# Half of the first feed-forward chunk placed inside the last attention step, with key-tile sums on GpSimd in every step

## The reference

```python
qkv = einsum('bsd,ed->bse', x, w_qkv) + b_qkv
scores = einsum('bhqd,bhkd->bhqk', q, k) / sqrt(32) + causal
out = softmax(scores) @ v                       # heads joined, 512 wide
x = layernorm(x + out @ w_out.T + b_out)
hidden = relu((x @ sign(up_weight).T) * up_scale)           # 2048 wide
x = layernorm(x + (hidden @ sign(down_weight).T) * down_scale * output_scale)
```

## Time and profile before

| | us |
|---|---|
| three runs | 776.65, 772.4, 778.32 |
| median | 776.65 |
| the profiled execution, device time | 774.34 |
| its span | 772.6 |

### The profile page before, as it was taken

How to read it: one execution, slowest core, us unless ns; L and a number is a source line. 1 busy time by engine, 2 the same in 40 slices (tenths; PEclk the granted TensorE clock), 3 DMA queues, 4 the chain that set the end, 5 groups by cost and what they waited for, 6 DMA issues and landing times.

```text
span 772.6 us, 11683 instructions
## 1 busy us (share of the span) xinstructions
PE 722.7 (94%) x4032; PEld 505.2 (65%) x4032; DVE 450.5 (58%) x1086; ACT 317.2 (41%) x631; POOL 354.4 (46%) x487
## 2 busy tenths in 40 slices
PE   6899999999999999999979889999999999999993
PEld 4788665655656556565544544788778787878882
DVE  4176495785967859678567751633294339334515
ACT  5211365654655546555546565432232222122210
POOL 4461467394673946739423502632353235223333
PEclk9999999999999999999999999999999999999998
DMA  6976464435544355452677331313012001000101
GB/s 231 296 208 177 110 174 124 136 105 163 150 132 132 108 157 148 115 133 88 174 206 261 109 123 58 120 32 119 14 41 95 28 1 41 15 1 12 44 1 54
DMA packets 44619, 85.71 MB, mean 111 GB/s; under 512 B 4880, under 2 KB 13584, under 8 KB 44432
## 3 DMA queue, kind: packets, MB, share of 16 engines
q1 hardware_dynamic: 35536, 79.72, 34.2%
q10 hardware_dynamic: 9024, 5.24, 2.4%
HBM read 55.33 MB, written 29.36 MB: 110 GB/s over the span
## 4 chain that ended last, share of the span: by engine, by line
PE 71%; DVE 19%; issue 3%; DMA 3%; POOL 2%; ACT 2%; SPq 0%; ACTq 0%; POOLq 0%
PE ps_heads L1045 9%; PE ps_proj L1087 7%; DVE heads_sb L835 7%; PE ps_proj L947 7%; PE ps_score L1104 6%; PE ps_unit L1063 6%; PE ps_unit L1087 5%; PE ps_sum L1039 5%; DVE maxes L813 5%; PE ps_unit L983 4%; PE ps_heads L1104 3%; PE ps_unit L1015 3%; PE ps_sum L1104 3%; PE ps_score L1015 2%; PE ps_score L983 2%
## 5 line engine op out<-in xcount | busy, mean ns | idle before, releaser
L655 POOL TENSOR_TENSOR hid_low<-hid_raw,hid_high 128x512 fp32r<-128x512 f32 x64 | 85.1, 1330 | 175.0 <-DVE hid_high L886 171.9
L711 ACT ACTIVATE probs<-ps_unit 128x512 f32<-128x512 f32 (+3 forms) x216 | 101.9, 490 | 88.4 <-PE ps_unit L1015 85.0
L619 POOL TENSOR_SCALAR_AFFINE_SELECT probs<-probs 128x128 f32<-128x128 f32 x256 | 73.1, 298 | 113.0 <-ACT probs L711 108.9
L711 ACT ACTIVATE probs<-ps_score 128x512 f32<-128x512 f32 (+3 forms) x155 | 75.2, 498 | 77.0 <-PE ps_score L1015 75.6
L886 DVE CAST hid_high<-hid_raw 128x512 fp32r<-128x512 f32 x64 | 27.1, 424 | 125.4 <-ACT hid_raw L766 125.2
L809 DVE CUSTOM_DVE_ANT_0 ps_unit<-ps_unit,causal 128x512 f32<-128x512 f32 (+3 forms) x162 | 80.1, 511 | 32.5 <-PE ps_unit L983 31.5
L1045 PE MATMUL ps_heads<-probs,v_rows 128*32 128x512 f32 (+3 forms) x768 | 80.3, 502 | 11.8 <-DVE heads_sb L837 11.8
L983 PE MATMUL ps_unit<-stack 96*128 96x512 f32 (+3 forms) x246 | 83.8, 354 | 5.7 <-DVE maxes L809 2.5
L1015 PE MATMUL ps_unit<-stack 98*128 98x512 f32 (+2 forms) x216 | 78.4, 366 | 4.1 <-DVE maxes L809 4.0
L613 POOL TENSOR_TENSOR parts<-qk_full,parts 128x512 fp32r<-128x512 f32 x32 | 41.3, 1289 | 64.7 <-ACT parts L690 64.4
L835 DVE RECIPROCAL heads_sb<-ps_sum 128x128 f32<-128x128 f32 x64 | 60.8, 950 | 9.2 <-PE ps_sum L1039 9.2
(11 more groups left out here) (195 smaller groups left out, 1478.0 us busy)
## 6 DMA issues: line engine op xcount, KB each, us to landing
stack<-qk_parts SPq DMA_DIRECT2D x96, 256.0 KB, 4.6
qk_parts<-parts SPq DMA_DIRECT2D x32, 512.0 KB, 2.9
v_all<-h_even ACTq DMA_DIRECT2D x16, 256.0 KB, 3.8
v_rows<-v_all SPq DMA_DIRECT2D x8, 512.0 KB, 4.3
heads_t<-heads_sb SPq DMA_DIRECT2D x16, 256.0 KB, 3.4
raw<-up_w SPq DMA_DIRECT2D x8, 512.0 KB, 3.9
x_tile<-x_rows SPq DMA_DIRECT2D x16, 256.0 KB, 5.5
raw<-down_w SPq DMA_DIRECT2D x8, 512.0 KB, 3.4
```

Source lines behind the costliest of these rows:

```text
L655: nc.gpsimd.tensor_tensor(hid[1][:, (HM * s + n) % 3, :], hid_raw[:, n % 2, :], hid[0][:, (HM * s + n) % 3, :].bitcast(FP32), ALU.subtract ...
L711: nc.scalar.activation(probs[:, (NP * s + n) % RING, 0:width], bank(what, s, n)[:, off:off + width], ACT.Exp, scale=SCALE).then_inc(s_exp, 1)
```

## The change

Chunk 0 is worked in two rounds of two token tiles (256 tokens) each. Round 0 has its 16 up and 16 down tiles inside step 7, from slot 16 to 49.3, with its own small buffers for the hidden tiles (`hid0`); round 1 starts at the old place. To make room, the first two tiles' output projection moves into the end of step 6, the layer norm of chunk 0 to the front of step 7, the weights' loads are ordered up and down in turns, and step 7's scores have three PSUM banks up to piece 16 and two after it (four before). GpSimd adds the four full key tiles in steps 6 and 7 too. In step 6 the fetch of the heads, w_out and x stand ahead of the projection block (1, 3), whose twelve matmuls go from slots 11.9 to 17.1 to slots 19.4 to 26.2, with its store at 29.4 and its return at 31.9 (before: 19.9 and 22.2). The down weights are written into `down_sb` from above, as before, but their last two loads wait for the added tiles only.

```diff
@@ -36,10 +36,10 @@
 PAIRED = [13, 13, 19.6, 19.6, 28, 28, 36, 36, 44, 44, 52, 52]
 PAIRED_NORM = [19.7, 19.71, 19.72, 19.73, 52.05, 52.06, 52.07, 52.08]
-ALONE = [[11.2, 13.5, 15.7, 18.3, 24, 28, 31.5, 36, 39.5, 43, 46.5, 50.3],
+ALONE = [[11.2, 13.5, 15.7, 18.3, 28, 30, 32.2, 36, 39.5, 43, 46.5, 50.3],
          [10, 12.4, 15, 17.5, 24, 28, 31.5, 35, 38.5, 42.5, 46, 48.6]]
-ALONE_NORM = [[18.4, 18.41, 18.42, 18.43, 50.4, 50.41, 50.42, 50.43],
-              [17.6, 17.61, 17.62, 17.63, 48.7, 48.71, 48.72, 48.73]]
+ALONE_NORM = [[19.25, 19.26, 19.27, 19.28, 50.4, 50.41, 50.42, 50.43],
+              [17.6, 17.61, 17.62, 17.63, 55, 56.2, 57.4, 58.6]]
...
@@ -47,13 +47,11 @@
 BLOCK = [(1, 2, 0.5, 0.98, 13.05, 15.8, 18.5), (1, 3, 13.3, 0.5, 19.65, 22.4, 24.8),
          (2, 0, 20.5, 1.2, 34.4, 37.2, 40), (2, 1, 36.3, 0.6, 44.05, 46.8, 49.2)]
-LAST_BLOCK = [(1, 2, 4.2, 0.48, 9.9, 12.5, 14.9), (1, 3, 11.9, 0.45, 17.1, 19.9, 22.2)]
+LAST_BLOCK = [(1, 2, 4.2, 0.48, 9.9, 12.5, 14.9), (1, 3, 19.4, 0.62, 26.7, 29.4, 31.9)]
 FIRST_ADD, LAST_ADD = 4, 8
 NA = 3 * GH
-ADDING = STEPS - 2
...
+ROUNDS = [(0, (0, 1)), (0, (2, 3))] + [(i, tuple(range(TT))) for i in range(1, CH)]
+TILES = [0, 2, 4, 8, 12, 16]
+FILL_FROM = 17
+JOBS = [("out", 0), ("out", 1), ("up", 0), ("up", 1), ("down", 0), ("up", 2), ("down", 1), ("up", 3), ("down", 2), ("up", 4),
+        ("down", 3), ("up", 5), ("down", 4), ("up", 6), ("down", 5), ("up", 7), ("down", 6), ("down", 7)]
...
@@ -145,12 +151,11 @@
         paired = s < STEPS - 2
         for g, at in enumerate(PAIRED if paired else ALONE[s % 2]):
             put(t + at, "pv", s, g)
-            if g < FIRST_ADD or g >= LAST_ADD or s >= ADDING:
+            if g < FIRST_ADD or g >= LAST_ADD:
                 put(t + at, "sum", s, g)
-        if s < ADDING:
-            for a in range(NA):
-                put(t + 21.7 + 1.3 * a, "add", s, a)
-            put(t + 43.9, "sum_added", s)
+        for a in range(NA):
+            put(t + 21.7 + 1.3 * a, "add", s, a)
+        put(t + (43.9 if paired else 39.4 - s % 2), "sum_added", s)
         for q, at in enumerate(PAIRED_NORM if paired else ALONE_NORM[s % 2]):
             put(t + at, "norm", s, q)
             if q % 4 == 3:
@@ -181,50 +186,51 @@
     late = NP * (STEPS - 2)
     put(late + 30.5, "consts")
-    signs = [late + 23, late + 25.5] + [late + 29 + 4.6 * k for k in range(4)] + [late + 50.2 + 4.5 * k for k in range(4)]
-    signs += [late + 88, late + 92] + [FIRST_UP + 1, FIRST_UP + 3] + [FIRST_UP + 7 + 2 * k for k in range(4)]
+    last = NP * (STEPS - 1)
+    signs = [late + 31, late + 33.5] + [late + 37 + 3.6 * k for k in range(14)] + [late + 88.6, late + 91.4]
     for k, at in enumerate(signs):
-        put(late + 17.2 if k < 2 else signs[k - 2] + (3 if k < 4 else 0.5), "job", 0, k)
+        put(late + 28 if k < 2 else signs[k - 2] + 0.5, "job", 0, k)
         put(at, "sign", 0, k)
-    last = NP * (STEPS - 1)
-    put(late + 30, "fetch", 0)
-    put(late + 31, "fetch_x", 0)
+    put(late + 27.2, "fetch", 0)
+    put(late + 28.5, "fetch_x", 0)
     put(last + 12, "fetch", 1)
-    for i in range(4):
-        put(late + 38 + 2 * i, "split", 0, i)
-        put(late + 46.5 + 1.3 * i, "bias", 0, i)
+    for i in range(TT):
+        put(late + 36 + 1.7 * i, "split", 0, i)
+        put(late + 40 + 1.3 * i, "bias", 0, i)
         for m in range(12):
-            put(last + 0.5 + 5.2 * i + 0.42 * m, "attn", 0, 12 * i + m)
-        put(last + 5.8 + 5.2 * i, "y", 0, i)
-        put(last + 23 + i, "norm1", 0, i)
-        put(last + 26 + 2.5 * i, "turn", 0, i)
-    put(last + 22.5, "std1", 0)
-    for i in range(CH):
-        t = FIRST_UP + 16 * i
+            put((late + 44.5, late + 47.1, last + 2.5, last + 5.5)[i] + 0.22 * m, "attn", 0, 12 * i + m)
+        put((late + 47, last + 2.2, last + 7.7, last + 8.2)[i], "y", 0, i)
+        put(last + 9.4 + 0.1 * i, "norm1", 0, i)
+        put((last + 12.9, last + 13.4, last + 15.2, last + 15.7)[i], "turn", 0, i)
+    put(last + 9.3, "std1", 0)
+    for r, (i, tiles) in enumerate(ROUNDS):
+        t = FIRST_UP + 16 * (r - 1)
         for m in range(HM):
-            put(t + m, "up", i, m)
-            if i < CH - 1 or m < HM - 2:
-                put(t + m + 2.5, "down", i, m)
-        if i == CH - 1:
-            for q in range(TT):
+            put(t + m if r else last + 16 + 1.95 * m, "up", r, m)
+            if r < len(ROUNDS) - 1 or m < HM - 2:
+                put(t + m + 2.5 if r else last + 20 + 1.95 * m, "down", r, m)
+        if r == len(ROUNDS) - 1:
+            for q in tiles:
                 put(t + 17, "finish", i, q)
-        for q in range(TT):
-            put(t + 17.55, "z", i, q)
-            put(t + 18.6 + q, "ln2", i, q)
-            put(t + 19.5 + q, "out", i, q)
-        if i + 1 < CH:
+        end = t + 17.55 if r else FIRST_UP + 1.2
+        for q in tiles:
+            put(end, "z", i, q)
+            put(end + 1.05 + q, "ln2", i, q)
+            put(end + 1.95 + q, "out", i, q)
+        if r and i + 1 < CH:
             if i:
                 put(t - 4, "fetch", i + 1)
-            put(t + 0.5, "fetch_x", i + 1)
+            put(t + 0.2, "fetch_x", i + 1)
             for q in range(TT):
-                put(t + 2.2 + 0.7 * q, "split", i + 1, q)
-                put(t + 3 + q, "bias", i + 1, q)
+                at = 2 * q if i else 2.7 * q
+                put(t + (2.2 + 0.7 * q if i else 0.3 * q - 0.8), "split", i + 1, q)
+                put(t + (3 + q if i else 1 + q), "bias", i + 1, q)
                 for m in range(12):
-                    put(t + 5.2 + 2 * q, "attn", i + 1, 12 * q + m)
-                put(t + 6 + 2 * q, "y", i + 1, q)
-                put(t + 6.7 + 2 * q, "ln1", i + 1, q)
-                put(t + 7.4 + 2 * q, "turn", i + 1, q)
+                    put(t + (5.2 if i else 3) + at, "attn", i + 1, 12 * q + m)
+                put(t + (6 if i else 4.2) + at, "y", i + 1, q)
+                put(t + (6.7 if i else 5.1) + at, "ln1", i + 1, q)
+                put(t + (7.4 if i else 6.4) + at, "turn", i + 1, q)
...
-    order, had, users = [3, 4, 5, 0, 1, 2], {}, {}
+    order, had, users = [3, 4, 0, 1, 2], {}, {}
...
-            may = (2, 3, 4, 5) if s == STEPS - 1 else (0, 1, 2, 3, 4)
+            may = (2, 3, 4)[n >= FILL_FROM:] if s == STEPS - 1 else (0, 1, 2, 3, 4)
...
                         sp.wait_ge(s_wol, n - 1)
-                    if n < 2:
-                        src = w_out[:, n * 2 * HALF:(n + 1) * 2 * HALF]
+                    kind, k = JOBS[n]
+                    if kind == "out":
+                        src = w_out[:, k * 2 * HALF:(k + 1) * 2 * HALF]
                     else:
-                        src = (up_w, down_w)[(n - 2) // 8][(n - 2) % 8 // 2, :, (n % 2) * 2 * HALF:(n % 2 + 1) * 2 * HALF]
+                        src = (up_w if kind == "up" else down_w)[k // 2, :, (k % 2) * 2 * HALF:(k % 2 + 1) * 2 * HALF]
...
+                    parts2, full = hidden(s)
                     pool.wait_ge(s_hdh, HM * s + n + 1)
                     hidden_used(pool, HM * s + n - 2)
-                    nc.gpsimd.tensor_tensor(hid[1][:, (HM * s + n) % 3, :], hid_raw[:, n % 2, :],
-                                            hid[0][:, (HM * s + n) % 3, :].bitcast(FP32), ALU.subtract).then_inc(s_hdl, 1)
+                    nc.gpsimd.tensor_tensor(parts2[1][:, (HM * s + n) % 3, 0:tokens(s)], full[:, n % 2, 0:tokens(s)],
+                                            parts2[0][:, (HM * s + n) % 3, 0:tokens(s)].bitcast(FP32),
+                                            ALU.subtract).then_inc(s_hdl, 1)
...
-                        if s < ADDING and FIRST_ADD <= n < LAST_ADD:
+                        if FIRST_ADD <= n < LAST_ADD:
...
                     mm.then_inc(s_tt, 1)
                 if what == "up":
+                    i, tiles = ROUNDS[s]
                     if n == 0:
-                        pe.wait_ge(s_tl, TT * (s + 1))
-                    if s == 0 and n < 2:
-                        bank_read(last_user[(5, 2)[n]])
+                        pe.wait_ge(s_tl, TILES[s + 1])
+                    if s == 0 and n == 1:
+                        bank_read(last_user[2])
                     if s == 0:
-                        pe.wait_ge(s_sign, 3 + n // 2)
+                        pe.wait_ge(s_sign, JOBS.index(("up", n // 2)) + 1)
                     wait(pe, s_hr, HM * s + n - 1)
                     for m in range(2 * DC):
-                        mm = nc.tensor.matmul(ps_up[n % 2][:, :], up_sb[n // 8][:, n % 8, m % DC, :],
-                                              turned[s % 2][m // DC][:, m % DC, :],
+                        mm = nc.tensor.matmul(ps_up[n % 2][:, 0:tokens(s)], up_sb[n // 8][:, n % 8, m % DC, :],
+                                              turned[i % 2][m // DC][:, m % DC, columns(s)],
                                               start=(m == 0), stop=(m == 2 * DC - 1))
                     mm.then_inc(s_up, 1)
```

(18 more changed lines are left out.)

111 lines of the change are left out of this document (68 added, 43 removed).

## The result

| | median of the runs, us | ratio to before, 95% interval |
|---|---|---|
| before | 775.67 (20 runs) | |
| changed | 779.47 (20 runs) | 1.0057 [1.0041, 1.0073] |
| changed, run again | 780.01 (6 runs) | 1.0051 [1.0028, 1.0073] |

Forecast was 773.2. The kernel became 0.6% slower (3.8 us by the medians) instead of 0.3% faster: inside the range of 761 to 786 and within the 1% called no change, but on the other side. Two executions of the changed kernel were profiled. The first is the slowest of its 20 runs (span 781.5), the second lies on the fast side (span 776.1, 777.9 us of device time); where they differ, both numbers are given.

A forecast was written before the change was run, and what follows sets the result against it. PE was taken as the bound, with a late k1 costing most of the gain. Step 6 ending at 439.2, plus 66.6 for step 7, plus 292.2 less 28.8, gave span 769.2 (-3.4), median 773.2 us; range 761 to 786.

The forecast's parts named there:

- the sums' -5.3: Steps 6 and 7: three sum groups of 0.88 us fewer on the PE in each step, -5.3 us.
- k1's arrival: Step 6, SP's queue: k1, the 768 KB returned behind other loads, lands at 421.9; PE stands about 10 us at unit 32.
- rival C: Round 0's narrow ups: weight loads bound them at 0.19 us each instead of 0.12, +17.9, 791; chance 0.06.
- rival B: Step 7: GpSimd becomes the bound, each of ten downs one addition late, +12.9, 786 on the median; chance 0.11.
- From unit 32 to the end of the maxima ... 17.3: Step 6 behind the k1 wait: 17.3 us, of which one unused, so step 6 ends at 439.2.
- points the same way: Step 6: ACT, in order, waits for w_out from slot 31, landing at 409 to 411; no price given.
- What stays unused: ... I take 6.5: Step 7: 6.5 us of unused PE time on a demand of 60.1, making the step 66.6.
- Two table loads ..., half hidden, some 2: Step 7: two table loads of 1.28 us behind the moments, half hidden by two groups, leave some 2 us unused.
- -2.64 each: Steps 6 and 7: four sum groups of 0.88 us become one on the PE, -2.64 us per step.
- rival A: Step 6: transfers keep up, unit 32 runs at 410 to 411; span 758, -14.6, 762 on the median; chance 0.33.
- Without that wait it would end near 428: Step 6: without the wait for k1 the step ends near 428 instead of 439.2.
- the forecast case: Whole kernel with k1 late: own range 768 to 781, k1 at 416.3 to 427, step 7 unused 3 to 11; chance 0.50.

The follow-up runs named there:

- filler: Changed kernel plus 38 matmuls of 512 columns on the PE ahead of unit 32, whose results nothing reads; 777.5 us, ratio 1.0025.
- the edit of the standard deviation: First layer norm's standard deviation and its two table loads 1.5 slots later, on queue_best: 769.3 us, ratio 0.9910.
- the best order: queue_best with the standard deviation 1.5 slots later and the split of the heads' tiles at slots 38.5 to 42.4; 766.4 us, ratio 0.9866.
- k1_first: Changed kernel with k1's store right behind the heads' store and its return behind the first half of w_out; 777.7 us, ratio 1.0019.
- pe_sums: Changed kernel without GpSimd's additions in the last two steps, the PE summing all key tiles; 782.9 us, ratio 1.0099.
- loads_early: Changed kernel with k's last projection, store and return where they were before, w_out behind the projection, x and constants behind k's return; 773.8 us, ratio 0.9980.
- queue_best: loads_early with x, constants and two up weights behind the heads' fetch, and signs of up and down weights from slot 42; 774.8 us, ratio 0.9971.
- late_signs: k1_first with ScalarE's copies of w_out at slots 35 and 38 and its up and down signs from slot 42; 770.9 us, ratio 0.9953.
- loads_early_pe_sums: loads_early with the PE summing all key tiles in the last two steps, no GpSimd additions there; 773.2 us, ratio 0.9976.

## Why the prediction was wrong

The order of the queue was read rightly; the steps that failed are prices. The stretch behind unit 32 and the unused time of step 7 were both counted without the clock that falls at a wait of the PE, and the wait behind the table loads was taken as half hidden. Against the second profile these two make the miss of 6.9 us of span (2.5 in step 6, 4.7 in step 7); of the sums' -5.3 only the half in step 7 was there.

**Right:** k1's arrival (unit 32 at 423.8 and 420.3 for 421.9, a wait of 10.0 and 8.5 for "about 10"), ScalarE waiting for w_out ahead of it (4.65 us), rival C out by starts 0.12 apart, rival B out in step 7 (the one wait for a low part is 1.2 us), and everything from the first up of round 1 on: 263.4 forecast and measured.

**Wrong, step 6, "From unit 32 to the end of the maxima ... 17.3":** 24.2 and 21.1. I had measured the slow clock behind a gap of 4 us, and counted 1.2 us of it as going away, and then put a gap of 10 us into the same step at no price. The filler prices it at 1.6 to 4.7. The clock had fallen already at the wait for w_out ahead of it, which the prediction named as one that "points the same way" and gave no price either. The other 2.2 are two waits in the filler's trace, for `shift_l` (1.1) and for the bank of the output projection (1.2, DVE's `x_tile`).

**Wrong, step 7, "What stays unused: ... I take 6.5":** 10.1 and 11.2 on a demand of 60.1. "Two table loads ..., half hidden, some 2" was the term: the edit of the standard deviation alone gives 5.0 back and brings step 7 to 66.8, the forecast within 0.2. The loads hid nothing, since ScalarE stood 1.8 us for the moments first, and the clock fell behind the PE's wait. That 66.8 meets the forecast is in part luck: PE is idle 2.1 us of it and busy 64.7, where the prediction had 60.1 of demand and 1.9 for the changes of kind, so what it left for waits was too much and the demand too little.

**Wrong, the sums, "-2.64 each":** as taken from PE's work it came back as time in step 7 of the changed kernel alone (2.3 to 3.4 by the profiles), where PE is what is late. In the kernel before they cost 4.5 us, and 3.8 of it came back when the split was moved out of GpSimd's run. Rival B had this mechanism, with a cast and one addition; it looked for it in step 7 and for one instruction, and it was in step 6 and lasted a run of them. In the changed kernel the late k1 hid it: all but the last addition were over before the split began.

**Wrong, rival A, "Without that wait it would end near 428":** with k1 in time step 6 was 65.0, not 52.5. There were three more waits of ScalarE behind the same volume, one below the other. Even the best order has 58.0.

Term by term against the second profile (forecast in brackets): 375.2 to the start of step 6 (375.5), 66.2 (63.7), 71.3 (66.6), 263.4 (263.4), together 776.1 for 769.2; 2.5 of it are step 6 and 4.7 step 7. The first adds 4.6 in step 6: 1.5 until unit 32 and 3.1 behind it. One sum of the prediction does not fit its own words: the bounds that it names for the forecast case (k1 at 416.3 to 427, 3 to 11 us unused) give 764 to 783 together, not 768 to 781; the whole range of 761 to 786 holds both. Not settled is why executions of one kernel differ by as much as 5 us in their clock behind the same wait: in the first profile it stayed at 0.50 for 12 us behind unit 32, in the second for some 5.

## What to carry to other kernels

Price a wait of the PE at its length and the clock behind it: here 2 us less of waiting were worth 5.0 in the executions in which the clock fell, and 2.2 in one in which it did not. When a load is late, look which in-order engine asks for it, and what it withholds meanwhile; asking 4 slots later gave 6.8 us, after moving the load ahead had given 1.8. Work given to GpSimd should not form a run without gaps while DVE has an operation with two SBUF operands that someone waits for.

## What the runs showed of the hardware that was not expected

DVE's subtraction of two SBUF operands, 0.69 us by itself, took 5.31, 3.79 and 3.49 us beside GpSimd, and each time it ended 0.54 or 0.55 us after GpSimd's last instruction of an unbroken run. Three additions of 1.27 us were in the first, with masks between them. The Trainium skill, "SBUF — State Buffer", Who interferes with whom, gives the pair of ports to whoever issues first, for the whole instruction. The rows agree that it is exclusive; but DVE lost it to instructions that started up to 4 us after its own, so here the wait lasted through the run and not for one instruction.

38 matmuls on a bank that nobody reads brought the clock back: it was 1.00 in the 12 us behind a transfer that was waited for (0.50 and 0.81 without them), and the kernel was 1.9 us faster for 10.7 us of useless work. Whether the clock falls behind a wait is not fixed by its length: the 3.15 us wait of step 7 was followed by 10 us at 0.68 to 0.84 in seven profiles (both of the changed kernel, k1_first, filler, pe_sums, loads_early, queue_best), and at 1.00 in two (late_signs, loads_early_pe_sums).
